# First expert layer: another order around the expert tiles, the first batch's hidden layer in two halves, one shared expert of the fourth batch ahead of the tiles

## What is computed

```python
logits = (x @ wt.T + repeat(g @ wg.T, s)) / 2
scores = softmax(logits);  topk_w, topk_idx = top_k(scores, 2);  topk_w /= topk_w.sum(-1)
y_all  = einsum('etm,emh->eth', leaky(x @ w_gate[e]) * (x @ w_up[e]), w_down[e])   # 8 routed experts
y      = (y_all[topk_idx] * topk_w).sum(1)
p      = (leaky(x @ sw_gate) * (x @ sw_up)) @ sw_down                              # 2 shared experts
y      = y + p                                                                     # leaky(x) = max(x, 0.01 x)
h = silu(y @ w1.T * w1_s) * (y @ w2.T * w2_s)                                      # feed-forward, 1024 hidden
h = gelu(h @ h1.T * h1_s);  h = gelu(h @ h2.T * h2_s);  x = x + h @ w3.T * w3_s
```

## Time and profile before

| | |
|---|---|
| median of 3 runs | 2638.07 us (2637.86 to 2645.0) |
| profiled execution | 2652.06 us, of which the span is 2650.2 us |
| mean granted clock of PE in it | 0.967 |
| PE busy | 2507.8 us (95%) |
| DVE, ACT, POOL busy | 1417.1, 1071.4, 983.2 us (53%, 40%, 37%) |
| first expert block, from its first transpose to the first P7 | 919.09 to 1127.08 us |

### The profile page before, as it was taken

The page is one execution under the profiler, slowest core; times in us unless marked ns, Lnnn a source line. Parts: engine busy times, 40 slices in busy tenths (PEclk is TensorE's granted clock), DMA queues, the critical chain, the costliest instruction groups (busy, mean ns, idle before and its releaser), DMA issues. The chain is left out here.

```text
span 2650.2 us, 37857 instructions
## 1 busy us (share of the span) xinstructions
PE 2507.8 (95%) x13266; PEld 1552.1 (59%) x13266; DVE 1417.1 (53%) x3288; ACT 1071.4 (40%) x2618; POOL 983.2 (37%) x1028
## 2 busy tenths in 40 slices
PE   7999999899999899699999999999999899899998
PEld 4565655534343467387878777556656567544456
DVE  7466575467667353432424243565565578455555
ACT  4767676344544223111111111465666355112122
POOL 3655465178768324531212121765655200000000
PEclk9999999989999889799999999999999999999997
DMA  4000000000000146300000100432333000400000
GB/s 160 1 1 1 1 1 21 9 13 13 13 13 9 39 129 198 125 1 1 1 0 1 43 1 1 146 123 77 106 114 98 0 1 1 131 1 3 3 10 26
DMA packets 91518, 108.52 MB, mean 41 GB/s; under 512 B 16396, under 2 KB 72597, under 8 KB 91078
## 3 DMA queue, kind: packets, MB, share of 16 engines
q1 hardware_dynamic: 87606, 96.27, 11.5%
q0 software_dynamic: 3728, 9.83, 1.3%
HBM read 92.52 MB, written 9.35 MB: 38 GB/s over the span
## 5 line engine op out<-in xcount | busy, mean ns | idle before, releaser
L1014 POOL TENSOR_TENSOR cb_sc<-cb_toep,cb_mk 128x128 f32<-128x128 f32 (+3 forms) x256 | 215.6, 870 | 190.7 <-ACT cb_pr L1052 180.1
L1014 POOL TENSOR_TENSOR cb_bias<-cb_bias,cb_mk 128x128 f32<-128x128 f32 (+3 forms) x256 | 215.3, 871 | 148.6 <-DMA cb_bias<-in_fside_16xSxS 148.5
L1653 DVE TENSOR_REDUCE gb_bmax<-PS 128x8 f32<-128x512 f32 x256 | 164.5, 685 | 87.0 <-PE PS L1431 86.6
L398 PE MATMUL PS<-ident,cb_pr 128*128 128x128 f32 x1280 | 198.6, 284 | 4.0 <-ACT cb_pr L1052 2.3
L699 DVE CUSTOM_DVE_ANT_0 cb_sc<-PS,cb_sc,cb_sneg 128x128 f32<-128x128 f32 (+3 forms) x256 | 129.9, 547 | 125.0 <-PE PS L388 121.5
L398 PEld LDWEIGHTS PS<-ident,cb_pr 128*128 128x128 f32 x1280 | 135.3, 141 | 96.9 <-issue 82.7
L1812 ACT ACTIVATE gb_pt<-PS 128x512 f32<-128x512 f32 x256 | 139.4, 596 | 111.0 <-PE PS L1438 105.8
L1058 ACT ACTIVATE cb_pt<-PS 128x128 f32<-128x128 f32 (+3 forms) x448 | 163.6, 414 | 39.1 <-PE PS L398 38.6
L1431 PE MATMUL PS<-gb_ks,gb_qs 32*128 32x512 f32 x512 | 171.6, 668 | 8.0 <-DVE gb_bmax L1653 6.4
L699 DVE CUSTOM_DVE_ANT_0 cb_bias<-PS,cb_bias,cb_sneg 128x128 f32<-128x128 f32 (+3 forms) x256 | 129.3, 546 | 90.2 <-PE PS L388 89.3
L2347 PE MATMUL PS<-eb_g,ff_h 128*128 128x256 f32 x768 | 175.4, 382 | 0.0
(11 more groups left out here) (652 smaller groups left out, 5039.2 us busy)
## 6 DMA issues: line engine op xcount, KB each, us to landing
cb_bias<-in_fside_16xSxS SPq DMA_DIRECT2D x64, 256.0 KB, 2.9
cb_bias<-in_fside_16xSxS SPq DMA_DIRECT2D x64, 192.0 KB, 2.5
ff_h<-in_L_ffn_h_w SPq DMA_DIRECT2D x2, 4096.0 KB, 15.6
cb_bias<-in_fside_16xSxS SPq DMA_DIRECT2D x64, 128.0 KB, 2.2
y_rows<-eb_g SPq DMA_DIRECT2D x19, 256.0 KB, 2.2
cb_toep<-rel_table SPq DMA_DIRECT2D x8, 512.0 KB, 7.4
cb_bias<-in_fside_16xSxS SPq DMA_DIRECT2D x64, 64.0 KB, 2.2
ff_w<-in_L_ffn_w_w SPq DMA_DIRECT2D x3, 1024.0 KB, 8.3
```

The lines of the kernel that those rows point to most:

```text
L398: ins = pe.transpose(PS[:, bank, j * P:j * P + P], pr[:, v % 2, e, j * P:j * P + P], ident)
L1014: ins = pool.tensor_tensor(biases(v, e), turned(h, n) if L0 else biases(v, e), mk[:, b % 2, packed(t):packed(t) + n], ALU.add)
L1653: dve.tensor_reduce(bmax[:, n % 2, t, g + e, 0:NB], PS[:, bank + e, :].rearrange("p (n k) -> p n k", k=64), AX.X, ALU.max)\
```

## The change

All of it lies in `first_experts`.

- PE: `into(0, 0)` and `into(0, 1)` move from behind `logits(3)` to behind `logits(0)` and `logits(1)`. `ranks` goes between the gate and the up product of (1, 1). `into(3, 0)` comes behind `rows_of_slots`, ahead of the tiles. The second pair's transposes follow the first pair's products.
- Leaky of (0,0) to (2,1): ACT writes 0.01 x into `lk` and relu(0.99 x) into `gs`, POOL adds the two. Only (3,0) and (3,1) are made as before, by DVE.
- The multiply by the column in `hot_tiles` goes from DVE to POOL, with a semaphore each way. `rows_of_slots` on DVE goes ahead of `experts_of_tiles`, and `products` are moved to other places of the chain.
- First batch: `combine(0)` in two halves of 256 tokens, each followed by its own transposes and its own 8 x (w1, w2) products of 128x256. The gathers of a batch are issued by halves.
- A second buffer `yg1` (where the table L was) takes batch 1's rows, so batch 1's gathers wait for nothing and batch 2's wait for batch 0. The combines of batches 1, 2 and 3 move to the second half's m = 2 and m = 6 and to batch 1's m = 1 (before: batch 0's m = 3, 4, 6).
- POOL: batch 3's gathers go behind the S tables of group 0; S3 of each step is made in two halves of 1024 columns.
- ACT: an Exp and a Silu on two scratch numbers, so that their tables are there earlier. `turned` has two banks rather than four.

```diff
@@ tensor_program
                 logits(0)
+                into(0, 0)
                 turn_x(2, 0)
                 turn_x(2, 1)
                 logits(1)
+                into(0, 1)
                 turn_x(3, 0)
                 turn_x(3, 1)
                 logits(2)
                 logits(3)
-                into(0, 0)
-                into(0, 1)
                 into(1, 0)
                 down(0)
+                into_one(gates, "gate", 1, 1)
                 ranks()
-                into(1, 1)
+                into_one(ups, "up", 1, 1)
                 into(2, 0)
                 down(1)
                 into(2, 1)
                 rows_of_slots()
+                into(3, 0)
                 down(2)
...
-                into(3, 0)
                 into(3, 1)
                 down(3)
-                turn_y(0)
-                for b in range(B):
+                turn_first_y(0)
+                first_hidden(0)
+                first_hidden(1)
+                feed_forward(0)
+                for b in range(1, B):
+                    hidden(b)
                     feed_forward(b)
+                def first_hidden(half):
+                    for c in range(DC):
+                        turned_y.wait_emptied(pe, (0, c, half))
+                    if half == 0:
+                        pe.wait_ge(sm["ff_in"], 16 * 6)
+                    for m in range(FC):
+                        if half == 0 and m == 5:
+                            turn_first_y(1)
+                        for ring, name in ((gates, "w1"), (ups, "w2")):
+                            item = (name, 0, m) if half else (name, "half", m)
+                            bank = ring.put(pe, item)
+                            for c in range(DC):
+                                ins = pe.matmul(PS[:, bank, 0:HS], wf[name][:, c, m * P:m * P + P], yT[:, c, half * HS:half * HS + HS],
+                                                start=(c == 0), stop=(c == DC - 1))
+                            ins.then_inc(ring.filled(item), 1)
@@ vector_program
                 copy_logits(1)
+                products(0, 0)
                 copy_x(3)
-                copy_logits(2)
                 dve.wait_ge(sm["mo_const"], 16)
                 link(dve.tensor_copy(tri, tri32))
+                copy_logits(2)
+                products(0, 1)
                 copy_logits(3)
                 shifted()
-                products(0, 0)
                 pick_first()
-                products(0, 1)
                 pick_second()
                 products(1, 0)
                 sums()
                 slots_of_tokens()
+                products(1, 1)
                 hot_tiles()
-                products(1, 1)
                 hot_slots(0)
                 hot_slots(1)
+                products(2, 0)
+                rows_of_slots()
+                products(2, 1)
                 experts_of_tiles()
-                products(2, 0)
-                products(2, 1)
-                rows_of_slots()
+                leaky(3, 0)
+                products(3, 0)
                 weights_of_tokens()
...
-                products(3, 0)
+                leaky(3, 1)
                 products(3, 1)
+                combine(0, (0, 1), "mo_half")
+                copy_first_y(0)
+                for m in range(FC):
+                    gated_half(m, 0)
+                    if m == 3:
+                        combine(0, (2, 3), "mo_y")
+                    elif m == 4:
+                        copy_first_y(1)
                 for b in range(B):
...
                     for m in range(FC):
-                        gated_rows(b, m)
+                        if b:
+                            gated_rows(b, m)
+                        else:
+                            gated_half(m, 1)
                         if m == 5:
                             first_sums(b, 1, 0)
                             third_sum(b, 1, 0)
-                        if b == 0 and m in (3, 4, 6):
-                            combine({3: 1, 4: 2, 6: 3}[m])
+                        if b == 0 and m == 2:
+                            combine(1, range(NT), "mo_y")
+                        elif b == 0 and m == 6:
+                            combine(2, range(NT), "mo_y")
+                        if b == 1 and m == 1:
+                            combine(3, range(NT), "mo_y")
@@ scalar_program, gate_copy
-                    act.activation(gs[:, e, :], PS[:, bank, :], ACT.Copy).then_inc(gates.emptied(("gate", b, e)), 1)
+                        ups.wait_emptied(act, ("up", b - 1, e))
+                    if b < B - 1:
+                        act.activation(lk[:, e, :], PS[:, bank, :], ACT.Copy, scale=0.01)
+                        ins = act.activation(gs[:, e, :], PS[:, bank, :], ACT.Relu, scale=0.99)
+                    else:
+                        ins = act.activation(gs[:, e, :], PS[:, bank, :], ACT.Copy)
+                    ins.then_inc(gates.emptied(("gate", b, e)), 1)
@@ pool_program
+                def leaky(b, e):
+                    gates.wait_emptied(pool, ("gate", b, e))
+                    pool.tensor_tensor(lk[:, e, :], lk[:, e, :], gs[:, e, :], ALU.add).then_inc(sm["mo_lk"], 1)
+
+                def return_rows(b):
+                    if b > 1:
+                        pool.wait_ge(sm["mo_y"], b - 1 if b == 2 else b)
+                    for half in range(2):
+                        for k in range(2):
+                            for t in (2 * half, 2 * half + 1):
+                                n, at = k * NT + t, k * NJ + b * NT + t
+                                pool.indirect_dma_start(yg(b)[:, n, :], None, y_rows,
+                                                        bass.IndirectOffsetOnAxis(ap=slot_at[:, at:at + 1], axis=0))\
+                                    .then_inc(dyn[f"yg_in{n}"], 16)
+
+                for b, e in ((0, 0), (0, 1), (1, 0), (1, 1)):
+                    leaky(b, e)
+                pool.wait_ge(sm["mo_tile_hot"], 1)
+                pool.tensor_tensor(Hd[:, :, 1, :], Hq, column.unsqueeze(2).to_broadcast([P, 2 * NJ, TILES]),
+                                   ALU.mult).then_inc(sm["mo_column"], 1)
+                leaky(2, 0)
+                leaky(2, 1)
                 pool.wait_ge(sm["mo_rows"], 16)
...
+                return_rows(0)
+                return_rows(1)
+                return_rows(2)
                 for n in range(4 * B):
                     step, x = n // 2 % 2 + 1, n % 2
-                    if n in (0, 2):
+                    if n == 1:
+                        return_rows(3)
+                    if n < 4:
                         pool.wait_ge(sm[f"ff_h{step}in"], 16)
-                        h = wf[f"h{step}"]
-                        pool.tensor_tensor(h[:, 0:KH, S:2 * S], h[:, 0:KH, 0:S], h[:, 0:KH, S:2 * S],
+                        h, part = wf[f"h{step}"], slice(S + HS * x, S + HS * x + HS)
+                        pool.tensor_tensor(h[:, 0:KH, part], h[:, 0:KH, HS * x:HS * x + HS], h[:, 0:KH, part],
                                            ALU.subtract).then_inc(sm["st_S3"], 1)
```

More of the change, by code:

```diff
@@ L2291, in pair_out, with turn_first_y @@
                     ins.then_inc(pair_y.filled(("y", i)), 1)
+                def turn_first_y(half):
+                    pe.wait_ge(sm["mo_y" if half else "mo_half"], 1)
+                    for c in range(DC):
+                        bank = turned_y.put(pe, (0, c, half))
+                        for e in range(2):
+                            ins = pe.transpose(PS[:, bank, e * P:e * P + P], yr[:, 2 * half + e, c * P:c * P + P], ident)
+                        ins.then_inc(turned_y.filled((0, c, half)), 1)
                 def turn_y(b):
@@ L2439, in tensor_program @@
                 for i in range(PAIRS + 2):
-                    if i + 1 < PAIRS:
+                    if 1 <= i and i + 1 < PAIRS:
                         turn_rows(i + 1)
@@ L2568, in products @@
                                              op1=ALU.max).then_inc(sm["mo_lk"], 1)
+                def products(b, e):
                     bank = ups.take(dve, ("up", b, e))
-                    dve.wait_ge(sm["mo_lk"], n + 1)
+                    dve.wait_ge(sm["mo_lk"], 2 * b + e + 1)
                     if b > 1:
@@ L2606, in combine, with copy_first_y, gated_half @@
                             link(ins)
-                    ins.then_inc(sm["mo_y"], 1)
+                    ins.then_inc(sm[done], 1)
+                def copy_first_y(half):
+                    bank = turned_y.take(dve, (0, 0, half))
+                    dve.tensor_copy(yT[:, 0, half * HS:half * HS + HS], PS[:, bank, 0:HS]).then_inc(turned_y.emptied((0, 0, half)), 1)
+                def gated_half(m, half):
+                    item = lambda name: (name, 0, m) if half else (name, "half", m)
+                    bank = ups.take(dve, item("w2"))
+                    gates.wait_emptied(dve, item("w1"))
```

(15 more changed lines are left out.)

108 lines of the change are left out of this document (63 added, 45 removed).

## The result

The changed kernel takes 2625.46 us (median of 5 runs, 2622.26 to 2628.5), the one before 2638.07 beside it (5 runs, 2637.26 to 2645.0): a ratio of 0.9936, 95% interval 0.9922 to 0.995. It is faster, by 12.6 us of medians; 2617.6 was forecast. The profiled executions are 26.6 us apart (2652.06 and 2625.46; spans 2650.2 and 2623.5).

What follows compares the result with a forecast made beforehand. PE, busy 95% of the span, was taken as the bound, losing time to gaps and half clock. Front 1.4 and tail 19.05 sum to 20.5 us off the median of 2638.07, giving 2617.6, range 2604 to 2629.

Steps and rivals of the forecast that it cites:

- The tail: From the tiles' end to the first P7: 65.05 us against 84.1, so 19.05 less.
- The new wait: Second half of batch 0's hidden products: PE waits 6.9 us, combine(1) on DVE being held up by POOL's S tables.
- The wait for T2: At P6 behind the hidden products: T2 done at about 62, 1 us before P6's second half wants it.
- The front: Routing ahead of the tiles, through the tiles' end: the tiles end 1.4 us earlier.
- T0: End of the last logits, 942.5, which is 5.1 us later than before; bounds 940 and 952.
- The chain: DVE's routing from pick_first to POOL's first gather: 26.6 us against 27.85, first gather issued at 970.6.
- POOL's column multiply: In the routing chain, on 1248 bf16 elements: 2.9 us, between 1.45 and 4.5, holding up hot_slots throughout.
- The Relu: ACT's gate copies: two of 0.60 us, no table load; rival that Relu loads a table: gain 11, chance 0.03.
- No collision: Rival in the tail: POOL's S tables miss combine(1), stall 0.3 instead of 6.9, gain 29.9, 2608; chance 0.2.
- The late front: Rival: half clock through both early into and all logits, T0 = 952, gain 11, 2627; chance 0.12.
- The split buys nothing: Rival on batch 0's halves: fourth gather lands as late as the eighth, gain 16, 2622; chance 0.05.
- Slower through the clock in the tiles: Rival: clock falls at PE's wait for rows_of_slots and the tiles' transposes keep it at half, up to 2647; chance 0.03.

Runs made afterwards that it cites:

- no_collision: Changed kernel with combine(1) moved from the second half's m = 2 to behind the last T sums of step 1; ratio to the kernel before 0.9902, repeated 0.9896.
- start c: Label for profiles where PE waits 1.1 to 1.4 us for the shared expert's weights ahead of into(0, 0), the clock falling there or just before.
- start a: Label for profiles where the clock falls only at the end of the first logits or behind them, as in the profile of the kernel before.
- joined_early: Changed kernel with combine(1) behind the third sum, combine(2) behind P1's first evictions, both column multiplies on DVE; ratio to the kernel before 0.9875.
- group 1: First four follow-up kernels, on one chip with the kernel before beside them; there the unchanged kernel before had ratio 1.0001, the changed kernel 0.9924.
- group 3: Third four follow-up kernels, on a third chip with the kernel before beside them; there the changed kernel, nothing left out, had ratio 0.9915.
- column_on_dve: Changed kernel with both column multiplies on DVE and no semaphore to POOL; ratio to the kernel before 0.9917.

## Why the prediction was right, and what it mis-sized

**The tail (19.05 forecast, 20.5 measured).** Step by step, in us behind the tiles' end:

| | forecast | measured |
|---|---|---|
| the fourth gathered rows | 14.3 | 13.7 |
| first transpose of y | 15.0 | 14.3 |
| first hidden products | 16.7 | 15.9 |
| wait for the gated chunk | 6.9 | 7.12 |
| its end | 51.0 | 50.1 |
| rest of the hidden products | 7.15 | 6.68 |
| first P7 | 65.05 | 63.67 |

The new wait was forecast in its place, with its length and its cause, and no_collision shows that cause. The wait for T2 that was to be hidden by 1 us was hidden: P6 has no gap, nor has the second group's. 0.9 of the missing 1.4 us was there before the wait ended, 0.6 of it in gathers that landed earlier, and 0.5 is less half clock. The tails of the three profiles of the changed kernel agree (63.67, 63.92, 63.84).

**The front (1.4 forecast, 3.2 to 3.4 measured).** The mis-sized term is T0, the end of the last logits. 23.4 us behind the first transpose were forecast, 20.4 measured. I had them partly at half clock, as in the earlier trace rows. But the first `into`, 5.34 us against 3.68 at full clock, had brought PE to full clock before the second logits, and all later ones ran at it. Of these 3.0 us, 1.2 were given back on the way. The tables were ready 25.1 us behind T0, not 26.6, but PE's wait of 2.43 for them let the clock fall, which had stood at nothing in the sum, and 1.5 went there: these two cancel, by luck. 0.2 went in the copy ahead of the first pair's products. 0.8 went behind them: until the second pair's products start are 3.3 us (975.78 to 979.09), where the sum comes to 2.5, since eight transposes and a wait of 0.44 for ACT's copy stand between. And what the sum left out altogether is start c: the landing of the weights was not looked up for the moved `into`. In the profile after they had just been in time (the last load of them was issued at 921.3, such a load took 2.9 at the median, and the products start at 924.26); with the wait the front is 123.8, and nothing is left of the front's gain against a kernel before with start a.

The chain itself was near. From `pick_first` to the first gather are 26.2 us, against 26.6, and its parts are those named:

```profile
943.63 0.92 DVE L2528 TENSOR_TENSOR ff_h<-ff_h,eb_pm 128x128 f32<-128x128 f32 x1
950.16 1.14 DVE L2559 TENSOR_TENSOR eb_sa<-eb_nt,ff_h 128x64 f32<-128x64 f32 x1
955.78 2.67 DVE L2577 TENSOR_SCALAR ff_h<-ff_h 128x1248 bf16<-128x1248 bf16 x1
958.49 6.51 DVE L2581 TENSOR_TENSOR ff_h<-ff_h,eb_lo 128x2048 bf16<-128x2048 f32 x2
```
```profile
955.83 2.28 POOL L3053 TENSOR_TENSOR ff_h<-ff_h 128x1248 bf16<-128x1248 bf16 x1 [4.61 <-DVE ff_h L2574]
967.60 1.18 POOL L3062 DMA_INDIRECT eb_g<-x_rows,eb_row_at  x1 [4.75 <-DVE eb_row_at L2593]
```

Two small instructions wait about 0.6 and 0.9 us for an addition of POOL (0.29 and 0.23 alone). POOL's column multiply took 2.28, between the bounds of 1.45 and 4.5 and below the 2.9 taken. I had it hold up `hot_slots`; it held DVE's own multiply, issued at the same time, first (2.67, where it is 0.55 in the kernel before). The prediction had it right that the move of that multiply costs. joined_early shows the price, 1.4 us of PE's wait, and 1.7 of clock where that had not fallen before. The Trainium skill, SBUF — State Buffer, "Who interferes with whom", names `tensor_scalar` too, beside the instructions with two SBUF inputs, as one that can take the port pair shared with GpSimd. The trace agrees, with 2.67 us against 0.55.

**The Relu.** ACT's two copies of a gate, in the profile after:

```profile
930.57 0.59 ACT L2897 ACTIVATE eb_g<-PS 128x512 f32<-128x512 f32 x1
931.05 0.60 ACT L2898 ACTIVATE eb_g<-PS 128x512 f32<-128x512 f32 x1
```

No table load stands between or around them, as the Trainium skill, ScalarE: Activation LUTs, "Table sets: the hidden batching unit", has it. That rival is out.

**The other rivals.** "No collision" was priced at 9.6 us below the forecast. It did not come by itself, and made by an edit it brought 6.0 (group 1) and 7.2 of tail (group 3), since the collision moved on to `first_sums`. The late front didn't come, for the reason above. "The split buys nothing" is half true: with the collision there it was not tried; without it, the halves are worth 2.5 to 2.8 us. "Slower through the clock in the tiles" didn't come, though its first step did: the clock fell at the wait for the tables, but it was up again before the first pair (`down(2)` takes 3.62 at 970.79, the first eight products 1.99 at 975.78).

**The median.** The sum gave 20.5 us and the profiles show 23.8 at the same clock. The first comparison's 12.6 is less than either. That comes from its kernel before, not from the changed one, whose medians are 2625.46, 2623.01 and 2628.19: with 19 and 11 runs of it the medians differ by 23.2 and 19.6 us, and the ratios 0.9924 and 0.9915 stand beside the forecast's own, 2617.6 / 2638.07 = 0.9922. That they agree so closely is in part luck: the forecast reckons the front as 1.4 and nothing behind the first P7, and the executions of one kernel differ by more than that.

## What to carry to other kernels

When work moves on two engines that hold each other up, as VectorE and GpSimd did here, line up their blocks in time, not their sums. Beside a block of additions on GpSimd, VectorE here got one two-operand instruction done for each of GpSimd's (2.2 us each instead of 0.42), so put VectorE's two-operand work behind such a block. Then look for what is late next (here T2, then S2), and measure to a point behind that, not to the first one reached. Where a wait on TensorE is shortened or made, look at the clock behind it: the wait of 7.12 was followed by 2.3 us of loss, the one of 2.43 by 1.7 or by none. For work that is moved forward look up when its operands land, not only who computes them.

Before a gain of half a per cent is read off medians, compare the same stretch of the profiles at the same granted clock, and repeat the kernel before on the same chip: here its own spread was as large as the gain.

## What the runs showed of the hardware that was not expected

- The same kernel's front has two lengths, 3.3 us apart, by whether the granted clock falls within 1.6 us of the first transpose or 3 us later (123.87 and 127.20; 120.64 and 123.84). Ahead of them both PE timelines show the same gaps; what decides is not shown.
- A `tensor_scalar` of VectorE with one SBUF input, 128x1248 in bf16, took 2.67 us beside a GpSimd multiply of 2.28, and 0.55 without it. So not only instructions with two SBUF inputs are held, as the prediction had it.
- GpSimd is held too: its addition of 128x512, 1.27 us alone, took 3.21 beside VectorE's `hot_slots` in column_on_dve and joined_early.
- On one chip, ScalarE or VectorE stood for 3 to 7 us at the same two places in four different kernels, and of these the one that ran again on another chip didn't there. The group's kernel before was 8 to 10 us slower than elsewhere (2656.05 against 2646.23 and 2647.81). The cause is open.
